# Crossed last products, unpaused factor loads, new places, and five unread bfloat16 products a batch, in a two-layer transformer forward pass

## The reference

```
x = LN(x + L0_attn(x))           # Nystrom attention: 16 heads of 8, 64 landmarks, 6 Newton steps for an inverse
x = LN(x + L0_xattn(x, ctx))     # attention to ctx with a relative bias            (r1)
x = LN(x + L0_ffn(x))            # 8 experts, the best one of each row              (rm)
x = LN(x + L1_attn(x))           # causal attention, 16 heads of 8                  (r2)
x = LN(x + L1_xattn(x, ctx))     # masked attention to ctx, 16 heads of 64          (ry)
x = LN(x + L1_ffn(x))            # gelu, weights composed of 32 low-rank pairs      (rf)
```

## Time and profile before

| | |
|---|---|
| median of the runs | 2515.51 us |
| profiled execution | 2522.18 us |
| its span | 2520.2 us |
| mean granted TensorE clock | 0.953 |
| TensorE, VectorE, ScalarE, GpSimd busy | 90, 78, 58, 15% |

### The profile page before, as it was taken

One profiled execution on the slowest core, in us unless ns is written; L12 is line 12 of the kernel. 1 busy time (PEld: TensorE's weight loads), 2 busy tenths in 40 slices (PEclk: granted clock), 3 DMA queues, 4 the chain that ended last, 5 costly groups with the idle time before them and its releaser, 6 DMA issues.

```text
span 2520.2 us, 95538 instructions
## 1 busy us (share of the span) xinstructions
PE 2266.3 (90%) x40576; PEld 1846.1 (73%) x40576; DVE 1956.9 (78%) x6166; ACT 1450.1 (58%) x5093; POOL 387.1 (15%) x530
## 2 busy tenths in 40 slices
PE   6789999999999999999999999999999999999875
PEld 3677777777777777777777777777777777777764
DVE  3568888888888888788888888788888888888652
ACT  3346666656656655656656565665656566566531
POOL 2101111111111111111111111111111111111110
PEclk9889999999999999999999999999999999999885
DMA  4200000000000000000000000000000000000000
GB/s 192 90 7 9 5 7 9 9 9 9 9 5 7 9 9 8 9 5 8 8 9 9 9 9 5 8 8 9 9 9 9 5 7 9 9 9 8 6 3 2
DMA packets 29960, 35.75 MB, mean 14 GB/s; under 512 B 3544, under 2 KB 28128, under 8 KB 28384
## 3 DMA queue, kind: packets, MB, share of 16 engines
q1 hardware_dynamic: 29536, 29.65, 3.4%
HBM read 27.54 MB, written 2.10 MB: 12 GB/s over the span
## 4 chain that ended last, share of the span: by engine, by line
PE 52%; DVE 28%; ACT 15%; issue 4%; POOL 0%; DMA 0%; SPq 0%; POOLq 0%; DVEq 0%; ACTq 0%
PE ps L477 29%; PE ps L480 8%; ACT probs L1062 5%; PE ps L744 4%; DVE probsT L1349 3%; PE ps L828 3%; ACT probs L1047 3%; PE ps L876 2%; ACT ey L985 2%; DVE x_rows L1211 2%; DVE small L1252 2%; PE ps L761 2%; PE ps L665 2%; DVE qk_v L1337 1%; DVE p L1254 1%
## 5 line engine op out<-in xcount | busy, mean ns | idle before, releaser
L1102 POOL TENSOR_TENSOR small<-small,weights 128x1 f32<-128x1 f32 x256 | 149.0, 582 | 1142.7 <-DVE small L1200 1142.7
L1010 ACT ACTIVATE probs<-ps,small 128x128 f32<-128x128 f32 x1024 | 286.1, 384 | 31.0 <-DVE small L1342 29.5
L1349 DVE COPY probsT<-ps 128x512 f32<-128x512 f32 x384 | 263.1, 685 | 36.3 <-PE ps L480 32.7
L480 PE MATMUL ps<-weights,probs 128*128 128x128 f32 x1536 | 256.1, 292 | 32.8 <-ACT probs L1010 15.4
L1342 DVE TENSOR_REDUCE small<-ps 128x4 f32<-128x512 f32 x384 | 254.2, 683 | 20.5 <-PE ps L828 10.7
L1113 POOL TENSOR_TENSOR probs<-probs,small 128x256 f32<-128x256 f32 x128 | 108.7, 849 | 885.6 <-DVE small L1478 885.6
L480 PEld LDWEIGHTS ps<-weights,probs 128*128 128x128 f32 x1536 | 178.7, 146 | 86.3 <-ACT probs L1010 44.6
L929 ACT COPY x_T<-ps 128x128 f32<-128x128 f32 x128 | 34.1, 267 | 302.9 <-PE ps L480 302.9
L1062 ACT ACTIVATE probs<-ps,small 128x128 f32<-128x128 f32 x512 | 181.6, 375 | 20.5 <-DVE small L1342 19.0
L477 PE MATMUL ps<-wz,ss 64*64 64x72 f32 x6144 | 157.4, 229 | 32.5 <-DVE wz L1294 32.4
L1293 DVE SCALAR_TENSOR_TENSOR wz<-ey,ss 128x256 f32<-128x256 f32 x320 | 142.0, 444 | 51.1 <-ACT ss L970 36.9
(11 more groups left out here) (199 smaller groups left out, 5400.0 us busy)
## 6 DMA issues: line engine op xcount, KB each, us to landing
weights<-in_wpack SPq DMA_DIRECT2D x3, 1759.0 KB
fc_A<-in_b SPq DMA_DIRECT2D x2, 2048.0 KB, 14.3
fc_A<-in_a SPq DMA_DIRECT2D x2, 2048.0 KB, 11.4
x_in_T<-in_xT SPq DMA_DIRECT2D x32, 64.0 KB, 1.8
x_in_rows<-in_x SPq DMA_DIRECT2D x32, 64.0 KB, 1.8
ctx_T<-in_ctxT SPq DMA_DIRECT2D x32, 64.0 KB, 1.9
ctx_rows<-in_ctx SPq DMA_DIRECT2D x32, 64.0 KB, 1.9
mask_i<-in_mask SPq DMA_DIRECT2D x32, 64.0 KB, 1.9
```

Source lines behind the costliest of these rows:

```text
L480: return nc.tensor.transpose(dst, src, ident)
L1010: ins = nc.scalar.activation(probs(s, g)[:, j], bank(s, SCORE_BANK[g], 128 * j, 128), ACT.Exp, bias=sm(s, "nb", 4 * g + j, 1), scale=-1.0)
L1102: nc.gpsimd.tensor_tensor(sm(s, out), sm(s, ve), w("mhalf"), ALU.pow).then_inc(sem(done, s), 1)
L1349: V.tensor_copy(probsT(s, n % 4).rearrange("p a b -> p (a b)"), bank(s, 2)).then_inc(sem("pT", s), 1)
```

## The change

It has five parts. The products of `n.kk` (now one step, and one count of its semaphore in place of two), `n.W5` and `n.w` are crossed, and VectorE reads them from the swapped halves with one or two instructions more. Both sets of factors have buffers of their own, so the second load and the second scaling have no wait for the first composition; `f1` is in 32 pieces in place of 16, the scaling in four parts. The first projection no longer waits for the rows of `x`. `keep_busy` issues one bfloat16 product of 128 x 128 by 512 columns whose result nothing reads, ahead of each of the four `values` of `r1` and of `y_values(2)`. All places are new (PERIOD 74.45336 becomes 74.52428; the places of the lists below are shown for TensorE in two stretches only, the other lists are changed in the same way).

```diff
@@ PLACES, "pe" (n stream: from n.e1T0 on; r1 stream: the first places)
-        "... n.e1T0 26.271  n.e1T1 26.637  n.kk0 26.638  n.kk1 27.564  n.y0 28.348  n.S0 30.103  n.W0 35.190 ..."
-        "... n.S5 64.843  n.W5 66.411  n.w 67.483  n.o 70.169  n.z 70.352  n.out 75.641  n.ln 80.473  ",
-        "... r1.t0 100.534  r1.t1 102.791  r1.v0 103.035  r1.v1 106.840  r1.s23 109.249 ..."
-        "... ry.t2 214.518  ry.t3 215.616  ry.v2 218.183  ry.v3 219.221  ry.out 225.634 ..."
+        "... n.e1T0 26.692  n.e1T1 26.843  n.kk 27.896  n.y0 27.968  n.S0 28.491  n.W0 33.001 ..."
+        "... n.S5 60.934  n.W5 66.452  n.w 66.515  n.o 68.440  n.z 69.786  n.out 72.326  n.ln 76.093  ",
+        "... r1.t0 101.681  r1.t1 102.548  r1.v0 103.981  r1.v1 103.982  r1.s23 106.939 ..."
+        "... ry.t2 209.964  ry.t3 216.094  ry.v2 216.715  ry.v3 218.140  ry.out 223.113 ..."
@@ START
-        "load -1000.0000  factors 62.1304  "
+        "load -1000.0000  "
-        "... f1.15 62.1294  f2.0 81.0288  f2.1 87.1288 ... f2.15 143.7884  "
+        "... f1.31 60.9344  f2.0 66.5154  f2.1 72.3264 ... f2.15 129.7304  "
@@ buffers
-            fa = sb("fc_A", [128, 8192], scope=factors)
-            fb = sb("fc_B", [128, 2048], scope=factors)
+            fa = [sb(f"fc_large{n}", [128, 8192], scope=factors) for n in range(2)]
...
+    small_at = [(pp[0], pT[0]), (ka[0][:, 0:8], ka[0][:, 8:16])]
@@ SyncE, start
-            sp.dma_start(xin[:], x[0]).then_inc(once("first_in"), 16)
+            sp.dma_start(xin[:], x[0]).then_inc(once("rows_in"), 16)
...
+            factor_loads(1)
             yield "load"
-            sp.wait_ge(once("composed"), 1)
-            factor_loads(1)
-            yield "factors"
@@ TensorE, nystrom
-                pe.wait_ge(once("first_in"), 16 * 3)
+                pe.wait_ge(once("first_in"), 16 * 2)
...
-            for c in range(2):
-                pe.wait_ge(sem("n_eT", s), at("n_eT", s, 3 + c))
-                for i in range(4):
+            pe.wait_ge(sem("n_eT", s), at("n_eT", s, 4))
+            for i in range(4):
+                for c in range(2):
                     for m in halves:
                         t = k2T[M * c:M * c + M, i, m]
                         mm = one(PS[s][m, 1 - c, M * i:M * i + M], t, t)
...
-                            mm = one(PS[s][halves[m if last else m ^ g], g, PW * i + a:PW * i + PW], ss[halves[m], p, 0:M],
+                            mm = one(PS[s][halves[m ^ g], g, PW * i + a:PW * i + PW], ss[halves[m], p, 0:M],
                                      wz[halves[m], p, a:PW])
...
-            for h in range(H):
-                _, _, p, m = heads(h)
-                mm = one(PS[s][m, 0, 16 * p:16 * p + HD], p2[m, p], ey[m, p, M:PW])
+            for i in range(4):
+                for g in range(2):
+                    p = 4 * g + i
+                    for m in range(2):
+                        mm = one(PS[s][halves[m ^ g], g, 16 * i:16 * i + HD], p2[halves[m], p], ey[halves[m], p, M:PW])
...
+        def keep_busy(to):
+
+            mmul(to.rearrange("p (a b) -> p a b", a=4), ident_bf[:], every(causal_bf[:], 4), start=True, stop=True,
+                 skip_group_check=True)
...
             def values(g):
+                if n_att == 1:
+                    keep_busy(bank(s, (0, 1, 1, 0)[g]))
                 pe.wait_ge(sem("pT", s), at("pT", s, n_p + g + 1))
...
             def y_values(g):
+                if g == 2:
+                    keep_busy(bank(s, g % 2))
                 pe.wait_ge(sem("pT", s), at("pT", s, g + 9))
@@ GpSimd, scale(n)
-                nc.gpsimd.tensor_tensor(small, small, over(mix_col[:, n], D), ALU.mult).then_inc(once("scaled"), 1)
+                for q in range(4):
+                    part_of = mixed[n][0][q // 2][:, 4 * (q % 2):4 * (q % 2) + 4]
+                    nc.gpsimd.tensor_tensor(part_of, part_of, over(mix_col[:, n, 4 * q:4 * q + 4], D), ALU.mult
+                                            ).then_inc(once("scaled"), 1)
@@ VectorE, nystrom
-                        ins = V.scalar_tensor_tensor(Y, src[:, :, M:PW], 0.25, uy[:, ps], ALU.mult, ALU.add)
+                        for to, at_ps in ((slice(0, 128),) * 2,) if g == 0 else zip(halves, halves[::-1]):
+                            ins = V.scalar_tensor_tensor(Y[to], src[at_ps, :, M:PW], 0.25, uy[to, ps], ALU.mult, ALU.add)
...
-            v = bank(s, 0, 0, 128).rearrange("p (a b) -> p a b", b=16)[:, :, 0:HD]
-            for m, half in enumerate(halves):
-                ins = V.tensor_tensor(w9[half, :, m, 0:HD], v[half], sm(s, "rd")[half].unsqueeze(2).to_broadcast([M, PAIRS, HD]),
-                                      ALU.mult)
+            for g in range(2):
+                v = bank(s, g, 0, 64).rearrange("p (a b) -> p a b", b=16)[:, :, 0:HD]
+                for m, half in enumerate(halves):
+                    ins = V.tensor_tensor(w9[half, 4 * g:4 * g + 4, m, 0:HD], v[halves[m ^ g]],
+                                          sm(s, "rd", 4 * g, 4)[half].unsqueeze(2).to_broadcast([M, 4, HD]), ALU.mult)
```

More of the change, by code:

```diff
@@ L72 @@
     "pe": (
[16 rows of a table removed]
[16 rows of a table added]
     ),
     "act": (
[11 rows of a table removed]
[11 rows of a table added]
     ),
     "pool": (
-        "n.lm0 29.381  n.lm1 35.740  n.out 97.819  ",
-        "r1.ctx 135.356  r1.out 154.543  rm.out 170.775  r2.xbo 198.249  r2.out 198.282  ry.stats 204.577  "
-        "ry.xbo 209.993  ry.p0 223.550  ry.p1 225.077  ry.p2 231.021  ry.p3 241.150  ry.out 247.791  "
-        "rf.out 257.508  ",
+        "n.lm0 -4.000  n.lm1 -1.330  n.out 58.869  ",
+        "r1.ctx 94.622  r1.out 120.494  rm.out 132.002  r2.xbo 146.479  r2.out 154.873  ry.stats 165.659  "
+        "ry.xbo 180.030  ry.p0 193.242  ry.p1 194.413  ry.p2 198.063  ry.p3 198.064  ry.out 212.105  "
+        "rf.out 229.329  ",
     ),
     "dve": (
[17 rows of a table removed]
[17 rows of a table added]
     ),
@@ L146 @@
     "pool": (
-        "scale0 36.0000  prepare 40.0000  scale1 60.0000  "
+        "scale0 -1.3200  prepare -1.3100  scale1 -1.3000  "
     ),
     "dve": (
-        "clear -1000.0000  mix -999.0000  col -998.0000  f1 63.6294  f2 145.7884  "
+        "clear -1000.0000  mix -999.0000  col -998.0000  f1 79.0660  f2 142.3448  "
     ),
@@ L310, in body @@
     (orow, z, zT, res, PS, sm, over, every) = (o[k] for k in "orow z zT res PS sm over every".split())
-    wpack, rows, b2, a1, b1, a2, b2w, fa, fb, mix, mix_col, mix_tmp, left = (
-        o[k] for k in "wpack rows b2 a1 b1 a2 b2w fa fb mix mix_col mix_tmp left".split())
-    mixed = [(fb[:].rearrange("p (c d) -> p c d", c=16), a1, fa[:].rearrange("p (c f) -> p c f", c=16), b1),
-             (fb[:].rearrange("p (c d) -> p c d", c=16), b2w, fa[:].rearrange("p (c f) -> p c f", c=16), a2)]
+    wpack, rows, b2, a1, b1, a2, b2w, fa, mix, mix_col, mix_tmp, left = (
+        o[k] for k in "wpack rows b2 a1 b1 a2 b2w fa mix mix_col mix_tmp left".split())
+    small_at = [(pp[0], pT[0]), (ka[0][:, 0:8], ka[0][:, 8:16])]
+    mixed = [(a, b, fa[n][:].rearrange("p (c f) -> p c f", c=16), d) for n, (a, b, d) in
+             enumerate(((small_at[0], a1, b1), (small_at[1], b2w, a2)))]
     def once(name):
@@ L437, in start @@
             sp.dma_start(b2s[0:EXPERTS], b2).then_inc(once("weights_in"), 16)
+            factor_loads(1)
             yield "load"
-            sp.wait_ge(once("composed"), 1)
-            factor_loads(1)
-            yield "factors"
         def factor_loads(n):
             small, small_src, big, big_src = mixed[n]
-            sp.dma_start(small, small_src).then_inc(once("small_in"), 16)
             for half in range(2):
                 c = slice(8 * half, 8 * half + 8)
-                sp.dma_start(big[:, c], big_src[:, c]).then_inc(once("factor_in"), 16)
+                sp.dma_start(small[half][:], small_src[:, c]).then_inc(once(f"small{n}_in"), 16)
+            for half in range(2):
+                c = slice(8 * half, 8 * half + 8)
+                sp.dma_start(big[:, c], big_src[:, c]).then_inc(once(f"large{n}_in"), 16)
         def rest(s):
@@ L897, in start @@
             small, _, big, _ = mixed[0]
-            pe.wait_ge(once("scaled"), 1)
-            pe.wait_ge(once("factor_in"), 16 * 2)
+            pe.wait_ge(once("scaled"), 4)
+            pe.wait_ge(once("large0_in"), 16 * 2)
             for c in range(16):
-                mm = mmul(PS[1][:, 0], small[:, c], big[:, c], start=(c == 0), stop=(c == 15))
-                if c == 15:
-                    mm.then_inc(once("composed"), 1)
-                yield f"f1.{c}"
-            pe.wait_ge(once("scaled"), 2)
-            pe.wait_ge(once("factor_in"), 16 * 4)
+                for half in range(2):
+                    f = slice(256 * half, 256 * half + 256)
+                    mm = mmul(PS[1][:, 0, f], small[c // 8][:, c % 8], big[:, c, f], start=(c == 0 and half == 0), stop=(c == 15),
+                              skip_group_check=True)
```

(20 more changed lines are left out.)

14 lines of the change are left out of this document (7 added, 7 removed), and 102 rows, old and new, of tables (PLACES, START).

## The result

The changed kernel takes 2591.34 us (median of 4 runs, 2584.88 to 2617.11), the kernel before 2515.08 beside it: a ratio of 1.0322, 95% interval 1.0251 to 1.0392. The forecast was 2490 with 2524 as its upper end, so sign and range are both wrong. The interval is wide because one of the four executions, 2617.11 us, has a granted clock of 0.941 where the others have 0.953 to 0.958.

A forecast was written before the change was run, and what follows sets the result against it. TensorE's order list was taken to pace the kernel. Falls -22.4, period -3, opening -3 and +3 held back gave -25 us, from 2515.5 to 2490; the 8-in-10 range was 2470 to 2524.

The forecast's parts named there:

- New places: TensorE's reordered steps: longer waits at n.y0 and n.w offset by other waits filled; 0, bounds -0.5 to +1.25 us a period.
- Crossed last products: Sets of n.W5, n.w and n.kk: 1.28 us a period less on TensorE, VectorE paying; bounds -1.3 to +0.3 us.
- Five products: Unread products ahead of r1.v0 to v3 and ry.v2: cost 0 to 1.3 us a period, taken as 0.9.
- What they buy: Clock falls removed over 29 periods: 19 of 27 at 1.18 us each, 22.4 us; bounds 0 and 32.0.
- B: Thin TensorE stretch r1.v2, r1.v3, n.S2, r1.ctxT, r1.z: some 11 clock falls behind it, all expected to go.
- A: Thin TensorE stretch r2.s01, n.ln, n.proj: some 9 clock falls behind it, 7 expected to stay.
- C: TensorE stretch n.W5, n.w, ry.v2, n.o with small products: some 7 clock falls behind it, 6 expected to go.
- Rival 4: New thin stretches take over the falls of B and C: some 20 falls, 2504 us; counted within the forecast's 0.60 chance.
- Opening and end: Opening, second factors not waiting: -3 us, bounds 0 and -6; end after the last n.o: 0, 3 either way.
- Rival 1: Lists cost more than the clock gives: both fillers missed, +1.25 us a period, +40, 2530 us; chance 0.17.
- Rival 2: The clock doesn't care for the products: 27 falls as before, 2510 to 2520, 2514 us said; chance 0.12.
- signs of being wrong: Falls stay at B, clock-1.00 periods over 73.6 us, or waits ahead of n.y0 and n.w 0.6 us longer, none shorter elsewhere.

The follow-up runs named there:

- e2: Changed kernel with all order lists and the PERIOD of the kernel before, its other edits kept: 2525.6 us, 1.0030 of the kernel before.
- e5: Changed kernel with r1.t1 put back between n.kk and n.y0, and ry.t3 between n.W5 and n.w: 2555.08 us, 1.0139 of the kernel before.
- e14: Changed kernel with only r1.t1 put back between n.kk and n.y0: 2560.04 us, 1.0146 of the kernel before.
- e15: Changed kernel with both steps put back as in e5 and the five unread products taken out: 2597.86 us, 1.0304 of the kernel before.
- e13: Kernel before with only TensorE's list changed: n.y0 ahead of r1.t1 and n.w ahead of ry.t3: 2570.18 us, 1.0197 of the kernel before.
- e8: Changed kernel with the old lists of TensorE and VectorE, the other engines' lists new: 2570.27 us, 1.0205 of the kernel before.
- e12: e5 with two more TensorE steps moved, r1.z ahead of ry.t0 and r.ln3 behind n.S0: 2581.93 us, 1.0244 of the kernel before.
- e3: Changed kernel with all old lists, as e2, but without the five unread products: 2523.07 us, 1.0011 of the kernel before.
- e4: Kernel before with only the five unread products put in at the same places: 2544.11 us, 1.0101 of the kernel before.
- e17: Kernel before with the opening's edits alone (own factor buffers, unpaused loads, f1 in 32 pieces, four-part scaling, first projection not waiting): 2522.53 us, 1.0012.
- e9: Kernel before with one unread product a batch ahead of the wait of r1.z: 2513.99 us, 0.9986 of the kernel before.

## Why the prediction was wrong, step by step

**The step that failed** is "New places": "So it is a swap, and I cost it at 0; bounds -0.5 to +1.25 a period." The lists cost 66 us (e2 against after). By the profiled executions: a mean period of 76.61 against 74.36 us, 29 times is +65, the opening -5, the end +1, together 62. Of the 65, 16 more falls at 1.18 are 19, and the other 46 are 1.6 us a period: plain periods of 75.2 on the mean where e2 has 73.6 (the shortest ones differ by 2.0). The upper bound, 1.25, was too small for two reasons.

First, the two swaps were priced by their own waits alone, and those grew by more than the 0.66 and 0.59 allowed (0.17 to 0.95 and none to 0.80). For the period the 0 was nearly right in the new lists: putting both steps back shortens the plain period by 0.2 us only (75.1 to e5's 74.87). What was left out is the clock. With the waits there, falls come behind them and more falls come after these: 26 falls and 36 us, nearly all of it from the hand-off `n.kk`, `n.y0` (e14), and only as long as the five products are in (e15). The price also depends on the list: in that of before (e13) the same swaps cost 48 us, most of it as period, which is the upper bound itself.

Second, the other steps of the lists were dismissed in a sentence ("shifted by some us, in the same succession"), and GpSimd's, whose places moved by 28 to 52 us, weren't mentioned. The lists of the engines must fit one another. With both steps back there is still 1.8 us of plain period over e2 (74.87 against 73.1; 1.5 by the means), and a single foreign list costs 86 us or more. With only ScalarE's, GpSimd's and SyncE's lists new the plain period is 1.65 longer (e8). It is tempting to say that this is the same loss; but e8 is itself a mixture of lists that weren't made for each other, so that isn't shown. Which steps make the 1.8 us stays open; ScalarE's and GpSimd's old lists, each alone in the changed code, weren't tried, and where I picked two steps by their waits (e12) the kernel got slower.

**Crossed last products.** Right in its size on TensorE (1.28 foreseen, 1.2 measured, 0.65 us a set), wrong in what it does: -1.28 + 0.3 a period was taken, 0 measured (e3 at 72.70). The hand-offs on either side took it up, as the new waits of e3 show. TensorE at 92% of a period was read as its list being "the thing that paces the kernel"; the chain had VectorE and ScalarE in it for 43%, and that was the number to weigh.

**Five products.** 0.9 us a period foreseen at an issue distance of 0.26; 0.32 measured. By the shortest plain periods they cost 0.4 to 0.6 (e2 against e3, e4 against before); by the means of all 29 periods, with the falls taken off at 1.18, 0.6 and 1.0. That is inside the bounds and near the 0.9.

**What they buy.** 19 falls foreseen. In the old lists they remove 6 (e3 to e2; 11 by the means, and 6 from before to e4): at B 9 become 5, just behind `n.o` 6 become none, at A 9 become 12. "I expect B to go" is thus wrong by half for the old lists; the waits behind the products there stay as they were (VectorE's `z` has 28.8 us over the run in e2 as before), which may be why. In the new lists no fall is left at B, as foreseen, but others stand at 35, 52 and 76. In the new lists the products remove 18 (9 by the means) and gain nothing that shows, in the mended ones 35 and gain 43 us. The mechanism is there; its worth depends on whether another thin stretch stands ready to take the fall over. That the prediction held each fall to be its own, removable one by one at 1.18 us, is the second wrong step: the price of one was right, the independence wasn't. Its reading of C also leaned on busy time too much: ahead of four of C's seven falls, those within 0.1 us of an `n.o`, TensorE was busy all of the 3.4 us. One of them, in the kernel before:

```profile
2070.30:2073.70 3.40, 3.40 (x85) 3.00 (x85) 2.50 (x10) 0.00 (x0) 0.55 (x1) 1.00 0.02 5
```

It was at the sets of `n.W5` and `n.w`, the small products that the prediction names as well. Rival 4 (falls move to new thin stretches) was right in kind and had the wrong sign of the sum.

**Opening and end.** -3 foreseen with -6 as bound, -5.7 measured in one execution with as many falls (14) as before up to there; unpaused loads alone give 2.5 without the falls (e17). The end is -6.5, outside the 3 either way, and has 7 falls fewer. Both are small beside the rest.

**The rivals.** Rival 1, "the lists cost more than the clock gives", is the outcome, past its own point of decision (75.1, where it said 73.6). Its cause, the two missed fillers, accounts for 36 of the 76 us, and by falls instead of the +1.25 a period that it named; its price of +40 for the lists falls short of their 66, since it held the falls fixed and left the rest of the lists out; and its total of 2530 is 61 us short, since it kept the whole gain from the clock. The prediction's own signs of being wrong came true: plain periods over 73.6, and waits 0.8 us longer ahead of `n.y0` and `n.w`. Rival 2 is excluded by e5 against e15 (42 falls against 81, 2555 us against 2598): the clock does care for the products.

## What to carry to other kernels

A kernel whose engines run fixed order lists is to be priced at every hand-off where a step is put straight behind the one it depends on: look what stood between, and count both the wait and the falls of the clock that may come with it. Take work off an engine only with the chain in view; 1.2 us less on a TensorE that is busy 92% of the period were worth nothing here. A remedy against falls of the clock may show nothing alone and much together with another (2592, 2591, 2598 and 2555 us), so test them together too. And count falls over many executions: a single one had 7 more than the mean of its kernel (e9) or 11 fewer (e8).

## What the runs showed of the hardware

- The granted clock fell behind stretches with no long wait. In the 3.4 us ahead of the 27 falls before and the 37 after, TensorE was busy 1.7 to 3.4 us, and its waits were at most 0.95 us long (1.30 ahead of one fall). This goes against the sentence of the Trainium skill (TensorE: Matmul & The Clock Gate, "Why this matters for your kernels") that puts such drops down to long idle gaps between bursts of matmuls: here the drops came without such gaps.
- One fall costs 1.18 us by the periods and 1.1 by the scatter of 74 executions, not the 1.7 that 3.4 us at half speed would lose.
- Falls can settle at one phase: in e13 one comes at the same place nearly every period, at periods of 75.0 and 75.1 us. In the kernel after they stand 17.1 and 23.9 us apart (35.4, 52.5, 76.4) when a period has three.
- A product of 512 bfloat16 columns takes 0.32 us to the next work when it stands alone between small float32 ones; a pair of such took 0.26 each.
